# Soft mixture of a vision block: one turned running maximum, logits evicted by ScalarE, slot inputs between the turned weights

## The reference

```python
logits = jnp.einsum('bnd,esd->bnes', x, phi)
dispatch = jax.nn.softmax(logits, axis=1)
combine = jax.nn.softmax(logits.reshape(B, N, E * S), axis=-1).reshape(B, N, E, S)
slots = jnp.einsum('bnd,bnes->besd', x, dispatch)
h = jax.nn.gelu(jnp.einsum('besd,edh->besh', slots, w1) + b1[None, :, None, :])
y = jnp.einsum('besh,ehd->besd', h, w2) + b2[None, :, None, :]
out = jnp.einsum('besd,bnes->bnd', y, combine)
```

## Time and profile before

| | |
|---|---|
| median of three executions | 916.26 us (914.36 to 916.26) |
| the profiled execution's own time | 910.88 us |
| its span, first to last instruction | 909.0 us |
| TensorE busy | 836.4 us, 92% of the span |
| VectorE, ScalarE, GpSimd busy | 459.0, 461.3, 180.4 us |
| mean granted TensorE clock | 0.992 of full |

### The profile page before, as it was taken

One profiled execution on the slowest core, in us unless ns is written; L12 is line 12 of the kernel. 1 busy time (PEld: TensorE's weight loads), 2 busy tenths in 40 slices (PEclk: granted clock), 3 DMA queues, 4 the chain that ended last, 5 costly groups with the idle time before them and its releaser, 6 DMA issues.

```text
span 909.0 us, 14872 instructions
## 1 busy us (share of the span) xinstructions
PE 836.4 (92%) x5384; PEld 675.3 (74%) x5384; DVE 459.0 (50%) x1025; ACT 461.3 (51%) x945; POOL 180.4 (20%) x257
## 2 busy tenths in 40 slices
PE   1989989989989899989988999989999899989998
PEld 1866866766776687878877599966998589975988
DVE  4878688688687643366655410264004530163001
ACT  5887677678578443246645333354343342453232
POOL 3050040031010022236302500034001420034000
PEclk9999999999999999999998999999999999999999
DMA  7010000000000000001003000000000000000000
GB/s 203 1 40 2 1 27 12 0 12 23 0 1 1 27 12 23 12 24 45 16 1 121 1 1 0 5 14 0 0 0 17 0 0 0 0 18 1 1 1 17
DMA packets 12710, 15.48 MB, mean 17 GB/s; under 512 B 5312, under 2 KB 10560, under 8 KB 12544
## 3 DMA queue, kind: packets, MB, share of 16 engines
q1 hardware_dynamic: 10656, 9.46, 3.4%
q0 software_dynamic: 2016, 5.51, 2.2%
HBM read 13.39 MB, written 1.57 MB: 16 GB/s over the span
## 4 chain that ended last, share of the span: by engine, by line
PE 75%; DVE 12%; ACT 5%; issue 5%; DMA 1%; SPq 0%; POOL 0%; DVEq 0%; ACTq 0%; POOLq 0%
PE ps L222 20%; PE ps L1554 14%; PE ps L1481 6%; PE ps L1207 5%; PE ps L1569 5%; PE ps L1125 4%; PE ps L1299 4%; PE ps L1105 3%; DVE area L276 2%; ACT area L912 2%; PE ps L1113 2%; PE ps L1085 1%; DVE dstat L772 1%; PE ps L1165 1%; PE ps L1511 1%
## 5 line engine op out<-in xcount | busy, mean ns | idle before, releaser
L222 PE MATMUL ps<-xs,ws 128*128 128x512 f32 x460 | 124.9, 416 | 5.7 <-DVE xs L503 3.7
L1554 PE MATMUL ps<-area 128*128 128x192 f32 x768 | 127.4, 326 | 0.0
L1554 PEld LDWEIGHTS ps<-area 128*128 128x128 f32 x768 | 124.8, 190 | 2.1 <-issue 0.5
L222 PE MATMUL ps<-ws,wx 128*128 128x512 f32 x480 | 116.1, 397 | 1.2 <-DVE ws L793 1.2
L1053 ACT ACTIVATE area<-ps,bcol 128x512 f32<-128x512 f32 x96 | 65.7, 688 | 86.6 <-PE ps L222 86.6
L804 DVE TENSOR_TENSOR area<-ps,area 128x384 f32<-128x384 f32 x32 | 17.9, 558 | 177.8 <-PE ps L1554 177.7
L222 PEld LDWEIGHTS ps<-ws,wx 128*128 128x128 f32 x480 | 89.3, 188 | 22.6 <-DVE ws L793 3.0
L222 PEld LDWEIGHTS ps<-xs,ws 128*128 128x128 f32 x460 | 86.0, 196 | 24.1 <-issue 6.4
L912 ACT ACTIVATE area<-ps,nm 112x196 f32<-112x196 f32 (+1 forms) x240 | 85.6, 440 | 19.5 <-DVE nm L638 19.5
L415 POOL TENSOR_TENSOR area<-area,dstat 128x512 f32<-128x512 f32 x32 | 32.9, 1040 | 271.4 <-DVE dstat L769 271.4
L638 DVE TENSOR_REDUCE nm<-ps 112x4 f32<-112x784 f32 (+1 forms) x72 | 62.7, 874 | 26.8 <-PE ps L1105 21.7
(11 more groups left out here) (177 smaller groups left out, 1373.7 us busy)
## 6 DMA issues: line engine op xcount, KB each, us to landing
stage<-in_wall POOLq DMA_DIRECT2D x42, 128.0 KB, 2.4
area<-in_w2e SPq DMA_DIRECT2D x1, 2304.0 KB, 8.3
out<-xres SPq DMA_DIRECT2D x4, 384.0 KB, 2.6
xres<-in_x SPq DMA_DIRECT2D x1, 1152.0 KB, 7.8
area<-in_wall SPq DMA_DIRECT2D x2, 512.0 KB, 5.7
area<-in_w2a SPq DMA_DIRECT2D x1, 576.0 KB, 3.7
room<-in_rel SPq DMA_DIRECT2D x4, 128.0 KB, 5.7
xres<-in_x SPq DMA_DIRECT2D x1, 384.0 KB, 3.2
```

What stands on the lines that cost most here:

```text
L222: last = mm(out_, l, r, start=n == 0, stop=n == len(pairs) - 1)
L1554: last = mm(ps[:, 4 + b, s * D:s * D + D], hTd[:, m, b * T + s * P:b * T + s * P + P], w2x[:, e * MC + m, :], start=m == 0, stop=m == MC - 1)
```

## The change

- Logit tiles 0 to 7 go to banks 4, 5, 0, 1, 2, 3, 4, 5. ScalarE evicts all eight; VectorE's four copies (761) are gone, and so is the semaphore `d_rv`.
- The eight turned logit tiles with their eight reductions and the last reduction are gone. Instead VectorE keeps a running maximum over the tiles, `larger`: seven tensor_tensor instructions that read `best` and a tile of `ct`, both in SBUF; `best` is the space of `bc`. Then TensorE turns `best` once (four transposes into bank 4), and VectorE reduces that once.
- TensorE's order is: logits 0 to 5, turned weights 0 and 1, logits 6, turned weights 2 and 3, logits 7. Then it waits for the copies of the first four turned tiles, and goes on with the four parts of half 0 of the slot inputs; between them stand turned weights 4, 5, and 6 with 7. Then `best` is turned, half 1 begins, and the spreading of `nrm` (into bank 5) stands between the parts of image 0.
- The turned weights 0 to 3 are copied by VectorE, 4 to 7 by ScalarE. The slot inputs use banks 0 to 3 for half 0, 6 and 7 for image 0 of half 1, 4 and 5 for image 1. `gated` stands in front of seven groups on TensorE instead of two.

```diff
-        pm = dstat[:, 3:5, :].rearrange("p a b -> p (a b)").rearrange("p (n s) -> p n s", s=ST)
+        best = bc
...
+        def logit_bank(s):
+            return (4, 5, 0, 1, 2, 3, 4, 5)[s]
+        def slot_bank(b, h):
+            return ((0, 6), (2, 4))[b][h]
         gate = [sem(f"gate_{n}") for n in ("pe", "dve", "pool")]
             def body_d(it, nxt):
-                for s in range(ST + 5):
...
+                def larger(s):
+                    if s == 1:
+                        V.tensor_tensor(best, ct[:, 0, :], ct[:, 1, :], ALU.max).then_inc(d_pm, 1)
+                    else:
+                        dve.wait_ge(d_pm, it * (ST - 1) + s - 1)
+                        V.tensor_tensor(best, best, ct[:, s, :], ALU.max).then_inc(d_pm, 1)
+                def least(s):
+                    dve.wait_ge(d_ra, it * ST + s + 1)
+                    V.tensor_reduce(ncm[:, 2 * s:2 * s + 2], ct[:, s, :].rearrange("p (b t) -> p b t", b=2),
+                                    AX.X, ALU.max, negate=True).then_inc(d_ncm, 1)
+                def inverse(v):
+                    dve.wait_ge(d_dt, it * ST + v + 1)
+                    V.reciprocal(rcs[:, 2 * v:2 * v + 2], csum[:, 2 * v:2 * v + 2]).then_inc(d_rc, 1)
+                def turned_weights(v):
+                    dve.wait_ge(d_dtr, it * ST + v + 1)
+                    V.tensor_copy(dd[:, :, :, v * P:(v + 1) * P],
+                                  ps[:, 6 + v % 2, :].rearrange("p (b j c) -> p b j c", b=2, c=P)).then_inc(d_de, 1)
+                least(0)
+                least(1)
+                inverse(0)
+                least(2)
+                inverse(1)
+                least(3)
+                inverse(2)
+                least(4)
+                inverse(3)
+                turned_weights(0)
+                turned_weights(1)
+                least(5)
+                inverse(4)
+                turned_weights(2)
+                turned_weights(3)
+                least(6)
+                inverse(5)
+                larger(1)
+                least(7)
+                inverse(6)
+                larger(2)
+                inverse(7)
+                for s in range(3, ST):
+                    larger(s)
+                dve.wait_ge(d_rt, it + 1)
+                V.tensor_reduce(nrm[:], ps[:, 4, :].rearrange("p (n c) -> p n c", c=P), AX.X, ALU.max, negate=True)\
+                    .then_inc(d_nm, 1)
                 dve.wait_ge(d_bt, it + 1)
-                V.tensor_copy(bc, ps[:, 4, :]).then_inc(d_bc, 1)
+                V.tensor_copy(bc, ps[:, 5, :]).then_inc(d_bc, 1)
                 for h in range(2):
                     for b in range(2):
                         dve.wait_ge(d_sh, it * 4 + 2 * h + b + 1)
-                        bank = 4 * h + 2 * b
+                        bank = slot_bank(b, h)
                         V.tensor_tensor(slot_cols(slots[1], b, h), ps[:, bank, :].rearrange("p (e s) -> p e s", e=2),
                                         slot_cols(slots[0], b, h).bitcast(F32), ALU.subtract)
                         V.tensor_tensor(slot_cols(slots[2], b, h)[R1:P],
             image_out(PAIRS - 1, 1)
             def body_d(it, nxt):
-                for s in range(ST + 4):
-                    if s < ST and s % 2 == 0:
+                for s in range(ST + 1):
+                    if s < ST:
                         act.wait_ge(d_l, it * ST + s + 1)
-                        A.activation(ct[:, s, :], ps[:, s % 4, :], ACT.Copy).then_inc(d_ra, 1)
-                    if 1 <= s <= ST:
+                        A.activation(ct[:, s, :], ps[:, logit_bank(s), :], ACT.Copy).then_inc(d_ra, 1)
+                    if 1 <= s:
                         v = s - 1
                         act.wait_ge(d_ncm, it * ST + v + 1)
                                                 bias=ncm[:, 2 * v + b:2 * v + b + 1],
                                                 accum_out=csum[:, 2 * v + b:2 * v + b + 1])
                         last.then_inc(d_dt, 1)
-                    if s >= 5 and s % 2:
...
+                for v in range(4, ST):
+                    act.wait_ge(d_dtr, it * ST + v + 1)
+                    A.activation(dd[:, :, :, v * P:(v + 1) * P],
+                                 ps[:, 6 + v % 2, :].rearrange("p (b j c) -> p b j c", b=2, c=P), ACT.Copy)\
+                        .then_inc(d_da, 1)
                 for h in range(2):
                     for b in range(2):
                         act.wait_ge(d_st, 1 + it * 4 + 2 * h + b + 1)
-                        bank = 4 * h + 2 * b
+                        bank = slot_bank(b, h)
                         A.activation(slot_cols(slots[0], b, h), ps[:, bank, :].rearrange("p (e s) -> p e s", e=2), ACT.Copy)
                         A.activation(slot_cols(slots[2], b, h), ps[:, bank + 1, :].rearrange("p (e s) -> p e s", e=2),
                                      ACT.Copy).then_inc(d_sh, 1)
                 pe.wait_ge(ln_split, it + (3 * PAIRS + 1))
-                def to_slots(b, h):
...
+                def to_slots(b, h, part):
+                    for j in range(2):
+                        last = mm(ps[:, slot_bank(b, h) + part, :], xn[:, 2 * b + j, part * P:part * P + P],
+                                  dd[:, b, j, 512 * h:512 * h + 512], start=j == 0, stop=j == 1)
+                    if part:
+                        last.then_inc(d_st, 1)
+                def logits(s):
+                    if s >= 6:
+                        pe.wait_ge(d_ra, it * ST + s - 5)
+                    product(ps[:, logit_bank(s), :], (CPHI + s * P, CPHI + s * P + P), xcols(0, N)).then_inc(d_l, 1)
+                def turn_weights(v):
+                    if v == 0:
+                        pe.wait_ge(o_res, 1 + 4 * PAIRS)
+                        pe.wait_ge(d_res, 1 + it * NT)
+                    pe.wait_ge(d_dn, it * ST + v + 1)
+                    if 2 <= v < 6:
+                        pe.wait_ge(d_de, it * 4 + v - 1)
+                    if v >= 6:
+                        pe.wait_ge(d_da, it * 4 + v - 5)
+                    for n in range(NT):
+                        last = tr(ps[:, 6 + v % 2, n * P:n * P + P],
+                                  dt_[:, v % 4, n // 2, n % 2 * P:n % 2 * P + P], ident[:])
+                    last.then_inc(d_dtr, 1)
+                for s in range(6):
+                    logits(s)
+                turn_weights(0)
+                turn_weights(1)
+                logits(6)
+                turn_weights(2)
+                turn_weights(3)
+                logits(7)
+                pe.wait_ge(d_de, it * 4 + 4)
+                for k in range(4):
+                    gated(pe, 0)
+                    to_slots(k // 2, 0, k % 2)
+                    for v in ((4,), (5,), (6, 7), ())[k]:
+                        turn_weights(v)
+                pe.wait_ge(d_pm, it * (ST - 1) + ST - 1)
+                for n in range(NT):
+                    last = tr(ps[:, 4, n * P:n * P + P], best[:, n * P:n * P + P], ident[:])
+                last.then_inc(d_rt, 1)
+                pe.wait_ge(d_da, it * 4 + 4)
+                gated(pe, 0)
+                to_slots(0, 1, 0)
                 pe.wait_ge(d_nm, it + 1)
                 for n in range(NT):
-                    last = tr(ps[:, 4, n * P:n * P + P], nrm[:, n:n + 1].broadcast_to([P, P]), ident[:])
+                    last = tr(ps[:, 5, n * P:n * P + P], nrm[:, n:n + 1].broadcast_to([P, P]), ident[:])
                 last.then_inc(d_bt, 1)
+                to_slots(0, 1, 1)
                 pe.wait_ge(d_bc, it + 1)
-                pe.wait_ge(d_de, it * 4 + 4)
...
+                for part in range(2):
+                    gated(pe, 0)
+                    to_slots(1, 1, part)
                 pe.wait_ge(ld_w2, 32)
                 pe.wait_ge(w_split, NCHUNK - QKV_CHUNKS)
```

More of the change, by code:

```diff
@@ L201, in build @@
             sem(n) for n in ("c_own", "c_on"))
-        d_l, d_ra, d_rv, d_rt, d_pm, d_nm, d_bt, d_bc, d_cs, d_ce = (
-            sem(n) for n in ("d_l", "d_ra", "d_rv", "d_rt", "d_pm", "d_nm", "d_bt", "d_bc", "d_cs", "d_ce"))
+        d_l, d_ra, d_rt, d_pm, d_nm, d_bt, d_bc, d_cs, d_ce = (
+            sem(n) for n in ("d_l", "d_ra", "d_rt", "d_pm", "d_nm", "d_bt", "d_bc", "d_cs", "d_ce"))
         d_ncm, d_dt, d_rc, d_own, d_dn, d_dtr, d_de, d_da = (
@@ L755, in body_d @@
             def body_d(it, nxt):
-                for s in range(ST + 5):
[L757 to L777, removed]
-                    if s >= 5 and s % 2 == 0:
-                        dve.wait_ge(d_dtr, it * ST + s - 4)
-                        V.tensor_copy(dd[:, :, :, (s - 5) * P:(s - 4) * P],
-                                      ps[:, 7, :].rearrange("p (b j c) -> p b j c", b=2, c=P)).then_inc(d_de, 1)
@@ L1475, in body_d @@
                 pe.wait_ge(ln_split, it + (3 * PAIRS + 1))
-                def to_slots(b, h):
-                    for part in range(2):
-                        for j in range(2):
```

(39 more changed lines are left out.)

6 lines of the change are left out of this document (1 added, 5 removed).

## The result

The changed kernel takes 886.84 us in the median (885.86 to 888.25, four runs), the kernel before 915.31 in the median of four. The ratio is 0.969, with a 95% interval of 0.9664 to 0.9715. The forecast was 889.7 us with a range of 884 to 898: right in direction, and 2.9 us too high.

A forecast was written before the change was run, and what follows sets the result against it. TensorE, busy 92% of the span, was taken to bound the kernel. Transposes (3.08 us a pass) and shorter waits cut a pass from 37.85 to 31.2 us, 26.6 in four: 916.26 - 26.6 = 889.7 us, range 884 to 898.

The forecast's parts named there:

- What bounds: Touched 37.85 us of each soft-mixture pass: TensorE bounds, 32.84 us its work, 5.01 us waits and refilling.
- The opening: From a pass's first logits to its slot inputs: 11.74 us instead of 18.24, with TensorE waiting 0.70 us.
- Behind the opening: Slot inputs to third expert product: later work hidden behind TensorE; touched part 31.2 us instead of 37.85, saving 6.65 a pass.
- the second refilling of 0.24: Last three parts of the slot inputs: 0.24 us of refilling left in from the kernel before (7.12 - 6.88).
- The running maximum: VectorE's chain at 0.72 us a link ends at 18.3, wanted at 20.61: hidden, 2.3 us of slack.
- The collision with GpSimd: Links 1 to 3 meet three GpSimd multiplications: 1.4 us of slack, costed at nothing; 5.6 us in all without slack.
- Gates: Five added gates on TensorE: taken as costing nothing; upper end 0.23 us each, 4.6 us in all.
- The additions: GpSimd's additions start at about 24.1 instead of 28.07; the next pair's norm waits about 1.3 us, not wanted until later.
- Rival a: Opening: VectorE and ScalarE keep their pace, some 2 us a tile; 902, or 904 if only transposes pay; chance 0.15.
- Rival b: Gates and collisions cost their upper ends, 4.6 or 5.6 us: 894 to 895; chance within the forecast's 0.77.
- Rival c: Running maximum sets the end and slows the kernel, from 2.5 us a link; 926 at 3 us; chance 0.03.
- Rival d: Change does nothing: waits return elsewhere, refilling at nine switches eats the transposes' 3.08 us a pass; chance 0.03.

The follow-up runs named there:

- links between: Kernel before in its old order, with only the running maximum turned once, its links between VectorE's per-tile work: 917.35 us, ratio 1.0044.
- links last: Kernel before in its old order with the running maximum, its seven links behind VectorE's last reduction and reciprocal, turn one step later: 898.17 us, ratio 0.9844.

## Why the prediction was right, step by step

- **What bounds.** Right. TensorE in the touched part of a pass; the other engines through the waits. With eight turns instead of one the period grew by 3.08 us, the price at which the prediction counted a transpose. Its list of TensorE's waits lacks two that the timeline of before has, 0.48 and 0.16 us ahead of turned logit tiles; no term rests on them.
- **The opening.** Forecast at 11.74, measured 11.70. The lags (times from an instruction's start to the start of the one that waits for it) and durations of the kernel before carried over: weights 2 forecast at 9.27, found at 693.30 - 684.05 = 9.25; copies on ScalarE forecast 1.47 apart, found 1.46.
- **Behind the opening.** Forecast 31.2, measured 30.92. The term that was mis-sized is the second refilling of 0.24, which I left in because gates and waits stand there: the last twelve matmuls take 5.17 us, 0.43 each, and there is none. With it and the opening's 0.04, three passes gained 6.93 and not 6.65, 0.84 together. The first gained 7.43, 0.78 more than forecast; 0.5 of that is luck, the clock, since its first ten matmuls, which the change doesn't touch, took 3.28 in this trace and 3.76 in that of before. That makes the saving 28.2 instead of 26.6. Of the other 1.2 us by which the forecast was too high, 0.95 is that the median of before is 915.31 with a fourth run and not 916.26, and 0.3 that the medians differ by 28.5.
- **The running maximum.** Hidden, as forecast, but with 1.2 us of slack instead of 2.3: the chain ended at 19.3, not 18.3. The collision with GpSimd that was costed at nothing is there on both sides. The Trainium skill ("SBUF — State Buffer", Who interferes with whom) says that a VectorE instruction with two SBUF inputs contends with a GpSimd instruction that reads SBUF; the trace of after agrees: links of up to 1.41 us in place of 0.69, multiplications of up to 1.48 in place of 1.04. The end of the chain that the prediction worked out with full waits, 20.1, was too late by 0.8.
- **Gates.** Nothing, as taken; shown by the run without them. That the lone instruction is read ahead, the reason given, no run shows.
- **The additions.** Forecast to start at 24.1, found at 708.01 - 684.05 = 23.96; that the next norm waits for them costs nothing: a period without its pass is 98.87 - 30.92 = 67.95 us, and 105.78 - 37.85 = 67.93 before.
- **The rivals.** Rival a (the pace of before stays) fell: the copies come 1.46 us apart. Its price for the transposes alone, 904, was wrong as well, and in both directions: in the old order the same removal gave 917.4 with the links between and 898.2 with the links last. The prediction took a removed piece of TensorE's work to be worth itself in any order; in the old order TensorE waits for VectorE, and it isn't. Rival b's two costs stayed small: nothing for the gates, and 1.1 us of the slack for the collision. Rival c's point of decision, 2.5 us a link, counted waits alone, and slowed the last five links alone. With twice the links (7.95 us for the last five pairs, 1.6 a pair) 6.33 of the 6.91 us were gone: the first two pairs had moved the start of the last five from 14.7 to 17.0 us into the pass, and the clock fell behind the wait. So with all seven links slow the point is nearer to 1.7 us a link, an estimate from that run, 1.59 and a fifth of the 0.58 us that were left. Rival d fell: no switch between turns and slot inputs shows any idle time in the chain.

So of the 6.91 us a period, 4.00 come from the running maximum with its links out of the way (before against links last) and 2.91 from the new order with its evictions; 0.18 of that at most is the evictions'. TensorE has the same work in the kernel with links last and in the kernel after, so the 2.91 are waits and what follows them: the waits in its timeline of the third pass add up to 2.97 us with the links last (3.48 before) and to 0.62 after. Which part of the order (the places of the turned weights, the banks, the spreading between two parts) brings how much of it wasn't taken apart further. That the interleaving itself is needed shows in the run with all turned weights first, at 3.60. The parts don't add up freely: the first is worth -0.45 with the links in another place.

## What to carry to other kernels

Ask of every instruction that is moved or added what stands behind it in its engine's queue and who wants that: seven links of a running maximum were hidden in one place and turned a gain of 4 us a pass into a loss in another. Removing work from the busiest engine is worth its time only where that engine doesn't wait; where it does, remove the wait first or the removed work comes back as idle time, and with it perhaps a lower clock. When one edit reaches a few stages of many, read the period of its loop from the trace: it told 0.2 us a pass apart where the median of a whole run spread by several.

## What the hardware showed unexpectedly

- **The clock falls behind broken waits, and not each time.** One kernel, with waits of 1.6, 0.7 and 0.6 to 0.8 us and short turns between them, ran on at 2.4 GHz in one execution and fell to 1.2 GHz for 3 to 7 us in each pass of another: 900.58 and 908.89 us. The changed kernel with 0.28 us of idle time in its opening kept the upper level through every pass but the start of the first.
- **VectorE and GpSimd hold each other up.** A maximum of two SBUF tiles takes 0.69 us alone and up to 1.41 beside a GpSimd multiplication in the trace of after (1.49 with the links last), and the multiplication goes from 1.04 to as much as 1.48 (1.49). Reductions of one SBUF tile, and copies from PSUM, kept their 0.69 and 0.68 us beside the same multiplication.
